# A vision tower block on one core: the key products are copied out of their banks by VectorE instead of ScalarE

## The reference, cut to what matters

```python
qkv = (x @ qkv_w.T).reshape(b, n, 3, HEADS, HEAD_DIM).transpose(2, 0, 3, 1, 4)
q, k, v = (qkv[0], qkv[1], qkv[2])
attn = jnp.einsum('bhqd,bhkd->bhqk', q, k) * scale
attn = attn + jnp.einsum('bhqd,qkd->bhqk', q, r_p_k) * scale
attn = jax.nn.softmax(attn, axis=-1)
out = jnp.einsum('bhqk,bhkd->bhqd', attn, v)
out = out + jnp.einsum('bhqk,qkd->bhqd', attn, r_p_v)
return out.transpose(0, 2, 1, 3).reshape(b, n, QKV_DIM) @ proj_w.T + proj_b
```

## Time and profile before

| | |
|---|---|
| median of 3 runs | 4240.48 us (4234.64 to 4243.27) |
| the profiled execution | 4242.51 us, its span 4240.8 us |
| PE busy / PEld busy | 4025.1 us (95%) / 3938.8 us (93%) |
| DVE busy | 2885.2 us (68%) |
| ACT busy | 2497.5 us (59%) |
| POOL busy | 1280.7 us (30%) |
| granted TensorE clock | 0.979 of full speed as a mean; 1.00 in the middle groups of the attention |
| one middle group of the attention | about 349 us |

### The profile page before, as it was taken

The page is one execution under the profiler, slowest core; times in us unless marked ns, Lnnn a source line. Parts: engine busy times, 40 slices in busy tenths (PEclk is TensorE's granted clock), DMA queues, the critical chain, the costliest instruction groups (busy, mean ns, idle before and its releaser), DMA issues. The chain is left out here.

```text
span 4240.8 us, 84769 instructions
## 1 busy us (share of the span) xinstructions
PE 4025.1 (95%) x28203; PEld 3938.8 (93%) x28203; DVE 2885.2 (68%) x7468; ACT 2497.5 (59%) x6686; POOL 1280.7 (30%) x1423
## 2 busy tenths in 40 slices
PE   4986799999999999999999999999999799999999
PEld 4886699999999999999999999999999799999999
DVE  4675566766666766676766676667666677777776
ACT  2554666666766666666676666666665344444443
POOL 1323322232232232223223223222222344444443
PEclk8998899999999999999999999999999899999999
DMA  8641100000000000000000000000000322222222
GB/s 188 141 114 48 36 1 1 1 25 1 2 24 2 1 2 24 1 1 24 1 1 25 1 1 2 24 1 1 13 1 1 92 93 93 93 91 87 82 90 90
DMA packets 88974, 161.67 MB, mean 38 GB/s; under 512 B 5706, under 2 KB 75937, under 8 KB 85055
## 3 DMA queue, kind: packets, MB, share of 16 engines
q1 hardware_dynamic: 85118, 152.66, 12.6%
q0 software_dynamic: 944, 2.42, 0.3%
q10 hardware_dynamic: 2576, 2.36, 0.2%
HBM read 127.82 MB, written 29.60 MB: 37 GB/s over the span
## 5 line engine op out<-in xcount | busy, mean ns | idle before, releaser
L637 POOL TENSOR_TENSOR att_prob<-att_prob,att_total 99x396 f32<-99x396 f32 x768 | 649.9, 846 | 2108.7 <-DVE att_total L869 2108.7
L877 DVE TENSOR_REDUCE att_npeak<-att_s 99x2 f32<-99x396 f32 x768 | 434.8, 566 | 449.4 <-PE att_s L1090 440.5
L718 ACT ACTIVATE att_probT<-att_t 99x396 f32<-99x396 f32 x768 | 384.1, 500 | 572.1 <-PE att_t L1056 566.7
L730 ACT ACTIVATE att_prob<-att_s,att_npeak 99x198 f32<-99x198 f32 x1536 | 636.6, 424 | 137.3 <-DVE att_npeak L877 135.4
L1073 PE MATMUL att_o<-att_probT,att_vx 99*96 99x198 f32 (+1 forms) x3072 | 653.5, 335 | 1.1 <-DVE att_rx L862 1.1
L1090 PE MATMUL att_s<-att_kx,att_qx 96*99 96x198 f32 (+1 forms) x3072 | 642.5, 332 | 5.2 <-DVE att_qx L821 2.2
L1278 POOL TENSOR_TENSOR ffn_hidden<-ffn_relu 128x384 f32<-128x384 f32 x462 | 425.3, 927 | 482.6 <-ACT ffn_relu L1307 480.6
L1090 PEld LDWEIGHTS att_s<-att_kx,att_qx 96*99 96x99 f32 (+1 forms) x3072 | 481.4, 166 | 12.4 <-issue 6.0
L1307 ACT ACTIVATE ffn_relu<-ffn_h 128x384 f32<-128x384 f32 x462 | 225.7, 489 | 448.4 <-PE ffn_h L1527 446.5
L1539 PE MATMUL ffn_y<-ffn_down,ffn_hidden 128*128 128x192 f32 x2772 | 487.3, 327 | 1.6 <-DVE ffn_hidden L1431 1.6
L1073 PEld LDWEIGHTS att_o<-att_probT,att_vx 99*96 99x96 f32 (+1 forms) x3072 | 469.5, 179 | 4.4 <-issue 1.4
(11 more groups left out here) (241 smaller groups left out, 8117.8 us busy)
## 6 DMA issues: line engine op xcount, KB each, us to landing
ffn_gates<-gate_rows SPq DMA_DIRECT2D x66, 768.0 KB, 5.5
tok_pixels<-in_x SPq DMA_DIRECT2D x24, 1568.0 KB
ffn_hid<-hidden SPq DMA_DIRECT2D x35, 288.0 KB, 3.0
att_xres<-hidden SPq DMA_DIRECT2D x8, 1188.0 KB
hidden<-att_xres SPq DMA_DIRECT2D x8, 1188.0 KB
ffn_acc<-hidden SPq DMA_DIRECT2D x33, 288.0 KB, 2.9
out_hidden<-ffn_acc SPq DMA_DIRECT2D x33, 288.0 KB, 2.4
hidden<-tok_rows SPq DMA_DIRECT2D x7, 1176.0 KB
```

What stands on the lines that cost most here:

```text
L637: nc.gpsimd.tensor_tensor(prob[:, i % 2, :, :], prob[:, i % 2, :, :], view(total[:, i % 2, :], [[1, 2], [0, NTOK]]), ALU.mult).then_inc(pr ...
L718: nc.scalar.activation(probT[:, i % 2, :], t_bank[0:HALF, 0:2 * NTOK], ACT.Copy).then_inc(probT_made, 1)
L730: ins = nc.scalar.activation(prob[:, i % 2, h, :], s_bank[i % 2][0:HALF, h * NTOK:(h + 1) * NTOK], ACT.Exp, bias=npeak[:, i % 2, h:h + 1], ...
L877: nc.vector.tensor_reduce(npeak[:, i % 2, :], s_bank[i % 2][0:HALF, 0:2 * NTOK].rearrange("p (h k) -> p h k", h=2), AX.X, ALU.max, negate= ...
```

## The change

The copies of the four key banks, two instructions per bank (64 partitions by 396 numbers each, into the two heads' places in `kx`), leave ScalarE's list and stand in VectorE's list, at the same place in the plan. TensorE's and GpSimd's lists stay as they are. One wait is added on VectorE ahead of its first such copy, for GpSimd's work on `kx` at the start of the stage; ScalarE had and keeps the same wait.

```diff
@@ ScalarE, job()
-                    if kind == "last" or (kind == "first" and 12 <= j < 16):
+                    if kind == "last" or (kind == "first" and (4 <= j < 8 or 12 <= j < 16)):
                         return
...
-                    elif j < 8:
-                        cols = slice((j - 4) * HC, (j - 3) * HC)
-                        nc.scalar.activation(kx[0:64, s, 0, cols], bank[0:64, 0:HC], ACT.Copy)
-                        ins = nc.scalar.activation(kx[64:128, s, 1, cols], bank[64:128, 0:HC], ACT.Copy)
@@ VectorE, job()
-                    if kind == "first" and 12 <= j < 16:
+                    if kind == "first" and 4 <= j < 8:
+                        cols = slice((j - 4) * HC, (j - 3) * HC)
+                        dve.wait_ge(full[k % RING], up_to)
+                        nc.vector.tensor_copy(kx[0:64, s, 0, cols], bank[0:64, 0:HC])
+                        ins = nc.vector.tensor_copy(kx[64:128, s, 1, cols], bank[64:128, 0:HC])
+                    elif kind == "first" and 12 <= j < 16:
@@ VectorE, ahead of the opening's jobs
+                dve.wait_ge(keys_made, 4)
                 for j in opening[TURN:]:
```

## The result

The changed kernel takes 4258.43 us (median of 6 runs, 4255.95 to 4260.95), the kernel before 4240.20 us (6 runs on the same chip): ratio 1.0045, 95% interval 1.0032 to 1.0057, so about 18 us slower. The forecast was 4246.7. The range of 4229 to 4262, wide because it took in both rivals, holds the time; the forecast's own range, 4236 to 4256, ends 2.4 us under it. The profiled execution spans 4256.5 us against 4240.8.

What follows compares the result with a forecast made beforehand. TensorE bounds the attention nearly everywhere, so only its waits cost. Turning stretches 15.9, pair 2 5.6, pair 0 and like places 1.9, opening 0.5, less 17.7 for ScalarE's waits: +6.2 us, 4246.7 us; range 4229 to 4262.

Steps and rivals of the forecast that it cites:

- the gain in steps 4 of pairs 1 and 3: TensorE's waits there for ScalarE's copy of the turned probabilities go whole, 17.7 us gained in all.
- The copies' own 565 ns: One 396-column key copy out of PSUM on VectorE was estimated at 557 to 565 ns, taken as 565.
- The banks that were costed at nothing: Banks copied where VectorE has room, such as the third and fourth of pair 5, cost nothing.
- a bank costs VectorE's queue 2 x (0.565 - 0.08) = 0.97 us: Two copies per key bank, each next one starting some 80 ns before the last ends: 0.97 us of queue.
- K0: First key bank, pair 5 step 0, ahead of `npeak` of step 1: nothing hides it, 0.97 us a stretch.
- K1: Second key bank, pair 5 step 2, delays `npeak` of step 3; after 0.30 us of room, 0.67 us.
- K3, pair 4 step 12: Fourth key bank, copied at pair 4 step 10; 0.63 us shows where TensorE already waits at step 12.
- pair 2: Step 14 waits for the chain through the third and fourth banks: 0.80 us, seven times, 5.6 us.
- pair 0: Step 14 there, and like places in the last group, costs 0.24 us; eight places, 1.9 us.
- The forecast's upper bound of 1.12 us a bank: Bank cost from the 635 ns of a 448-column add out of PSUM; gave +15 us, 4255 us.
- The slower rival: Turning stretch gives no idle time back: four whole banks, 3.9 us a stretch, 27.2 for 15.9; 4258 us; chance 0.30.
- The faster rival: Pipeline's step of distance swallows lateness except at pair 5's first bank: -10.4 us, 4230 us; chance 0.20.

Runs made afterwards that it cites:

- odd_pairs_only: Against the kernel before, VectorE copies only the 64 key banks made during pairs 1 and 3, ScalarE keeps the others; 4221.04 us, ratio 0.9961.
- no_k2k3_even: VectorE copies all key banks except the third and fourth made in pairs 0, 2 and 4 and the four among the turning jobs; 4222.93 us, 0.9960 of before.
- same_start: Changed kernel, but each bank's second copy reads and writes partitions 0 to 63, so the second head's keys are not computed; 4244.87 us.
- filled kernels: 16 identity transposes ahead of pair 5 step 2's turning, on the changed kernel (4263.84, 4259.25 us) or with only pair 5's first bank moved (4256.02, 4249.28).
- turning_only: Against the kernel before, VectorE copies only the 28 key banks made in pair 5 of the first seven groups, among the turning jobs; 4254.26 us.
- k0_more: Kernel before, with VectorE copying only pair 5's first key bank (seven banks), preceded by two extra 128-column copies from the same bank; 4260.74 us.

## Why the prediction was right or wrong

**Held.** The table of waits named the right places for the gain: the gain in steps 4 of pairs 1 and 3 was forecast at 17.7 us and is 17.7 in the profile, 18.2 in odd_pairs_only. The copies' own 565 ns was right. The banks that were costed at nothing cost nothing (no_k2k3_even), and those that were costed at something are the ones that cost. The way of reckoning held too, a bank's time in VectorE's queue less the room at its place: see below the table.

**Failed: "a bank costs VectorE's queue 2 x (0.565 - 0.08) = 0.97 us".** The 80 ns of overlap were taken from four 256-column copies that all start at one partition. A bank's second copy starts at partition 64, and the bank takes 1.17 us. This term is the step that failed. What was worked out from it was too small:

| place | forecast, at 0.97 | changed kernel, at 1.17 | same_start, at 0.96 |
|---|---|---|---|
| K0 | 0.97 us | 1.15 | 0.95 |
| K1 | 0.67 | 1.07 | 0.77 |
| K3, pair 4 step 12 | 0.63 | 0.71 | 0.33 |
| pair 2 | 0.80 | 1.25 | 0.80 |
| pair 0 | 0.24 | 0.42 | 0.08 |

The room is what a place's banks take in the queue less what they cost (K2 and K3 of pair 4 are two banks, as are those of pairs 0 and 2). It comes out nearly alike in the last two columns: 1.6 us in pair 4, where the prediction had 1.3; 1.1 in pair 2, as it had; 1.8 to 1.9 in pair 0, where it had 1.7. Behind K1 it is 0.10 to 0.19 us, where it had 0.30. The prediction measured this one from the end of GpSimd's product, 1490.53, to the first matmul of the turning, 1490.83. But the weight load stands ahead of that matmul and needs the product too; in the kernel before:

```profile
1490.66 0.51 PEld L1056 LDWEIGHTS att_t<-att_ident,att_prob 99*99 99x99 f32 x4
```

From 1490.53 to this line are 0.13 us.

With 1.17 us a bank, the prediction's own sum gives 3.07 us a stretch, 1.20 in pair 2 and 0.64 in pair 0, and +17.8 us in all. That is near the measured +18.2, but by luck in part: the clock, which it left out, costs 4.7 us, and the rooms in pairs 4 and 0 were larger than it had. It also counted eight places like that of pair 0; ten show a cost, eight in pair 0 and two in the last group.

same_start is the kernel that the prediction described, and its +5.6 us meets the forecast +6.2; but it has three falls of the clock in it and smaller costs in pairs 4 and 0, so part of that agreement is luck, errors that cancel. The forecast's upper bound of 1.12 us a bank was under the true 1.17 as well, since it had the overlap in it; it gave +15.

**Missing: the clock.** No term stood for it. The wait that the prediction itself put at "near 2.2 us" was long enough for TensorE's clock to fall: in same_start, where it is 2.2 us, it fell in 3 of 7 stretches, in the changed kernel, where it is 2.5, in 6. There the falls make 4.7 us of the 20.2 in these stretches, the share that the filled kernels take away.

**The slower rival** named 4258, which is the time measured, by luck: its mechanism is not there. It had K2 and K3 of pair 4 cost whole banks, 1.94 us; they cost 0.71 in each of seven groups, so VectorE's idle time there was room after all. **The faster rival** fails at K1: nearly all of its 1.17 us reaches TensorE (0.79 us of wait, 1.07 us of time).

Of the signs, the ScalarE wait, the copies' length, the new wait behind K1 (0.79 us) and the one at step 12 of pair 4 (1.08) came as written; behind K0 it was 2.5 us instead of 2.2, and at step 14 of pair 2 1.52 instead of 1.2. "I am wrong if TensorE's total for turning grows by over 35" did not come: it grew by 26.1 us on the weight loads.

## What to carry to other kernels

Before work moves to an engine, ask of each place, not of the mean: here 64 of 192 banks were worth 18 us and the rest cost about 34 in two kernels of their own, and the waits told which. Take the spacing of two instructions from a pair that also changes its start partition as the new one does, not from the nearest pair of the same operation. Measure the room at a place up to the first instruction that needs the result, the weight load here and not the matmul. Where a wait of TensorE grows from 1.3 us to 2 or more, as here, add what the lower clock behind it may cost; in this kernel that was as much again as the wait's own growth when K0 alone was moved.

## What the runs showed of the hardware that was not expected

- Two 396-column copies out of PSUM: 0.48 us apart when both start at partition 0, 0.57 when the second starts at 64, and 0.60 from there to the next one at 0.
- The granted clock fell to 0.50 behind single waits of TensorE of 2.05 us in 4 of 7 stretches and of 2.45 us in 7 of 7, and never at the 1.27 to 1.33 us of before. With K1 to K3 moved as well it came in 6 of 7 (changed kernel, 2.5 us), 5 of 7 (turning_only, 2.5 us) and 3 of 7 (same_start, 2.2 us), so the length of the wait is not all that decides. A fall costs 1.25 us where nothing else is late. Of all 32 falls in these stretches 27 lasted 3.4 us and five, two of the changed kernel's, two of k0_more's and one of turning_only's, 6.8 us, and those cost 1.3 to 1.6 us more. The five long ones began 0.7 us before to 0.02 us after the end of the wait, the 27 others 0.25 to 1.8 us after it.
- A fall can hide a later wait: in all six of the changed kernel's stretches with a fall TensorE was so late after K0 that K1's 1.07 us no longer showed, and four of them came to 2.5 us instead of 3.5. In the stretch of the fall shown above, the turning of step 4 starts 0.67 us after its scores, without a wait.
- 1.56 us of transposes that nobody needs, inside a wait of 2.5 us, kept the clock at 1.00 in all 28 stretches with it.
